# The product of values and attention weights moves from VectorE's part loop to GpSimd, one tile between every two gathers

## The reference

```python
k_e = k[src] + e                    # e = edge features @ We
v_e = v[src] + e
alpha = einsum('ehd,ehd->eh', q[dst], k_e) / sqrt(D)
a = exp(alpha - segment_max(alpha, dst)[dst])
attn = a / segment_sum(a, dst)[dst]
out = segment_sum(attn[:, :, None] * v_e, dst)
```

## Time and profile before

| | |
|---|---|
| median of 3 runs | 5776.57 us |
| profiled execution | 5767.75 us, span 5765.9 us |
| attention gathers begin, end | 1820.4 us, 3115.1 us |
| POOL busy | 3351.3 us (58%) |
| DVE busy | 3076.6 us (53%) |
| PE busy | 3952.0 us (69%), mean granted clock 0.79 |

### The profile page before, as it was taken

One profiled execution on the slowest core, in us unless ns is written; L12 is line 12 of the kernel. 1 busy time (PEld: TensorE's weight loads), 2 busy tenths in 40 slices (PEclk: granted clock), 3 DMA queues, 4 the chain that ended last, 5 costly groups with the idle time before them and its releaser, 6 DMA issues. The chain is left out here.

```text
span 5765.9 us, 96432 instructions
## 1 busy us (share of the span) xinstructions
PE 3952.0 (69%) x24005; PEld 3074.7 (53%) x24006; DVE 3076.6 (53%) x9411; ACT 1420.4 (25%) x3648; POOL 3351.3 (58%) x4762
## 2 busy tenths in 40 slices
PE   1000586779996666677666539998998777777774
PEld 0000353446666566666665526665666666666664
DVE  7887510121115578888887641123114566666667
ACT  0002100010003144454444340002002233333333
POOL 7778988840003888888886220000000688888887
PEclk6555798889998888998997669999999655555555
DMA  9961342346554676676776115544552333333332
GB/s 373 368 227 51 104 156 101 123 129 195 189 167 132 182 210 203 204 233 201 212 221 176 40 59 192 190 139 143 191 189 75 97 92 92 92 92 92 92 92 76
DMA packets 537349, 892.82 MB, mean 155 GB/s; under 512 B 92522, under 2 KB 392140, under 8 KB 530910
## 3 DMA queue, kind: packets, MB, share of 16 engines
q1 hardware_dynamic: 420894, 611.37, 33.0%
q0 software_dynamic: 106912, 224.30, 14.6%
q10 hardware_dynamic: 9376, 55.32, 2.6%
HBM read 732.14 MB, written 158.57 MB: 154 GB/s over the span
## 5 line engine op out<-in xcount | busy, mean ns | idle before, releaser
L381 POOL DMA_INDIRECT work<-tab_gate,src_col x832 | 798.1, 959 | 1272.4 <-DMA tab_gate<-logits 1138.0
L1222 POOL DMA_INDIRECT work<-tab_kv,src_col x832 | 848.5, 1020 | 758.4 <-DMA tab_kv<-hw 589.2
L829 PE MATMUL ps<-hw 128*128 128x384 bf16 x5096 | 873.6, 332 | 108.5 <-DMA hw<-d_adj 62.5
L829 PE MATMUL ps<-hw,work 128*128 128x384 bf16 x5096 | 865.7, 331 | 81.4 <-DMA work<-d_adj 81.4
L501 POOL DMA_INDIRECT d_adj<-logits,address x782 | 800.6, 1024 | 172.3 <-issue 163.7
L869 DVE TENSOR_TENSOR work<-work,ps 128x128 f32 (+1 forms) x208 | 59.8, 288 | 1486.1 <-ACT work L861 1466.0
L829 PEld LDWEIGHTS ps<-hw 128*128 128x128 bf16 x5096 | 504.0, 99 | 451.1 <-issue 62.6
L829 PEld LDWEIGHTS ps<-hw,work 128*128 128x128 bf16 x5096 | 504.5, 99 | 415.7 <-issue 95.8
L861 ACT ACTIVATE work<-ps 128x128 f32 x208 | 57.7, 278 | 1845.6 <-PE ps L829 1845.6
L1737 PE MATMUL ps<-logits,work 128*128 x1664 | 342.9, 329 | 212.5 <-ACT work L1705 210.5
L1737 PEld LDWEIGHTS ps<-logits,work 128*128 128x128 f32 x1664 | 325.7, 291 | 294.7 <-issue 294.7
(11 more groups left out here) (404 smaller groups left out, 7298.7 us busy)
## 6 DMA issues: line engine op xcount, KB each, us to landing
hw<-d_adj SPq DMA_DIRECT2D x104, 800.0 KB
work<-d_adj SPq DMA_DIRECT2D x104, 800.0 KB
d_adj<-acc SPq DMA_DIRECT2D x52, 1568.0 KB, 21.5
hw<-d_adj SPq DMA_DIRECT2D x104, 768.0 KB
work<-d_adj SPq DMA_DIRECT2D x104, 768.0 KB
work<-attr_dram SPq DMA_DIRECT2D x832, 64.0 KB
d_value<-work SPq DMA_DIRECT2D x208, 256.0 KB
hw<-d_value SPq DMA_DIRECT2D x208, 256.0 KB
```

Source lines behind the costliest of these rows:

```text
L381: pool.indirect_dma_start(rows[:, r * U + u, 0:width], None, table, bass.IndirectOffsetOnAxis(sources[:, at:at + 1], 0)).then_inc(rows_in[ ...
L829: last = nc.tensor.matmul(at, adj_half[2 * s + hf][:, k, :], xs[:, b, :], start=b == 0, stop=b == BLOCKS - 1)
L1222: pool.indirect_dma_start(rows[:, r * U + at % U, 0:KV], None, tab_kv, bass.IndirectOffsetOnAxis(src_col[:, at:at + 1], 0)).then_inc(rows_ ...
```

## The change

`weigh_dve` is gone. The product is made by `weigh_part` on POOL, in two forms: in the tail on a whole part as before, and inside `att_pool` on one tile (128x128) behind every gather. While part n is gathered, part n-39 is weighed: its first tile waits for `exp_ready` and `value_in`, the last one signals `msg_ready`. From part 39 on the product stands where the pause stood; parts 0 to 38 and part 207 have no part to weigh, and only the first 39 keep their pauses. PE waits for `msg_ready` in both places.

```diff
-        def weigh_dve(dve, of, turn, r):
-            at, wide = weighed(dve, of, turn, r)
-            nc.vector.tensor_tensor(at, at, wide, ALU.mult).then_inc(sem("msg_weighed"), 1)
-
-        ATT_FILLS = STEPS
+        def weigh_part(pool, m, tiles):
+
+            first, last = tiles
+            r = m % PARTS
+            k = stretch_of(m)
+            p = m - FIRST_PART[k]
+            if first == 0:
+                pool.wait_ge(sem("exp_ready"), FIRST_PIECE[k + 1])
+                pool.wait_ge(value_in[r], 16 * (m // PARTS + 1))
+            n = last - first
+            at = msg_att[:, r * U + first:r * U + last, 0:D].rearrange("p u (h d) -> p u h d", h=HEADS)
+            wide = part_weights(k, p // PARTS, p % PARTS)[:, first:last, :]
+            ins = pool.tensor_tensor(at, at, wide.unsqueeze(3).broadcast_to((P, n, HEADS, HEAD_DIM)), ALU.mult)
+            if last == U:
+                ins.then_inc(sem("msg_ready"), 1)
+
+        ATT_FILLS = WEIGH_BACK * U
 ...
-                    pool.wait_ge(sem("paced"), SPREAD + at)
-                    pool.memset(pause, 0).then_inc(sem("paced"), 1)
+                    if 0 <= m < TAIL_PART:
+                        weigh_part(pool, m, (u, u + 1))
+                    elif m < 0:
+                        pool.wait_ge(sem("paced"), SPREAD + paced)
+                        paced += 1
+                        pool.memset(pause, 0).then_inc(sem("paced"), 1)
 ...
-                pe.wait_ge(sem("msg_weighed"), m + 1)
+                pe.wait_ge(sem("msg_ready"), m + 1)
 ...
-                m, of, turn, rm = part_of(k, i, r, WEIGH_BACK)
-                if summed_in_loop(k, m):
-                    weigh_dve(dve, of, turn, rm)
```

More of the change, by code:

```diff
@@ L1215, in att_pool @@
+        ATT_FILLS = WEIGH_BACK * U
         def att_pool(pool):
+            paced = 0
             pool.wait_ge(sem("table_out"), KV_TABLE)
             for n in range(ALL_PARTS):
-                r = n % PARTS
+                r, m = n % PARTS, n - WEIGH_BACK
                 if n >= PARTS:
                     pool.wait_ge(sem("kv_done"), n - PARTS + 1)
-                for at in range(n * U, (n + 1) * U):
-                    pool.indirect_dma_start(rows[:, r * U + at % U, 0:KV], None, tab_kv,
+                for u in range(U):
+                    at = n * U + u
+                    pool.indirect_dma_start(rows[:, r * U + u, 0:KV], None, tab_kv,
@@ L1226, in att_pool @@
                 if n == PARTS - 1:
                     pool.memset(acc_flat[:], 0.0).then_inc(sem("sums_zeroed"), 1)
+            assert paced == ATT_FILLS
         def tail_pool(pool):
             for m in range(TAIL_PART, ALL_PARTS):
-                k = stretch_of(m)
-                at, wide = weighed(pool, k, (m - FIRST_PART[k]) // PARTS, m % PARTS)
-                pool.tensor_tensor(at, at, wide, ALU.mult).then_inc(sem("msg_ready"), 1)
+                weigh_part(pool, m, (0, U))
         def weights_act(act, m, of, turn, r):
@@ L1380, in sums @@
                 pe.wait_ge(sem("win_added"), (m - PARTS + 1) * U + TURN)
-                pe.wait_ge(sem("msg_ready"), i * PARTS + r + 1)
+                pe.wait_ge(sem("msg_ready"), m + 1)
                 pe.wait_ge(sem("msg_weights"), m + 1)
```

## The result

The changed kernel took 5862.07 us (median of four runs, 5858.7 to 5866.01), the kernel before 5778.57 us beside it (5767.75 to 5786.07). The ratio is 1.0146, 95% interval 1.0129 to 1.0164: slower, by 84 us where 25 were forecast, and 4 us above the range. The profiled execution's span is 5855.7 us, 89.8 longer than before. The gathers of the attention pass begin at 1821.0 and end at 3201.1 us, so the pass lasts 1380.0 us against 1294.7: 85 of the 90 us are in it.

A forecast was written before the change was run, and what follows sets the result against it. The prediction took POOL's own work to be the attention pass's length, with DVE waiting. Its terms, 24 - 20 + 25 - 4 = +25 us on a median of 5776.57, gave 5802 us; the range was 5735 to 5858 us.

The forecast's parts named there:

- rival 4: Attention pass: DVE was the bound, so its relief of 115 us would count; at most 38.5 us back, 5738 us; chance 0.03.
- POOL's pauses become products: POOL in the attention pass: 672 memsets of 0.329 us become products of 0.365 us, +24 us (bounds -43 and +68).
- Relief of the gathers: POOL's gathers: fewer are lengthened once DVE loses line 1211, -20 us (bounds -42 and 0).
- New collisions: POOL's products meeting DVE's two-input line 1408 wait 0.34 us on average, +25 us (bounds 0 and +92).
- Boundaries: Between stretches: a slower POOL loses its extra time out of its wait for DVE's scores, -4 us (-10 to 0).
- New waits: The product's two waits, ahead of the part's other gathers, cost nothing; +10 us if the cover is gone.
- Rival 3: Locked phases: line 1408 keeps falling on a product in each part, +92 in place of +25, 5869 us; chance 0.12.
- Rival 1: The small POOL product is cheap, 0.265 us with next to no fixed part: sum -42, 5735 us; chance 0.20.
- Rival 2: Even exchange: product 0.34 us, line 1211 to blame for most long gathers (-30): sum -2, 5775 us; chance 0.24.

The follow-up runs named there:

- x1: Kernel before, with 672 of its POOL pauses replaced by a 128x128 product on a spare buffer, DVE keeping its own product: 5885.56 us, ratio 1.0189.
- x2: Kernel before, with the same 672 pauses made longer memsets (128x364), about as long as the product: 5822.01 us, ratio 1.0079.
- x3: Changed kernel, with POOL's product in the pass on 64 of the 128 columns of a tile: 5803.18 us, ratio 1.0045.
- w2: Changed kernel, with one 128x512 product behind a part's last gather in place of four small ones: 5813.12 us, ratio 1.0063.
- y4: Kernel before, with 672 pauses replaced by copies of 128x128, on a slower chip: 6366.62 us, ratio 0.9861 to the kernel before there.
- x4: Changed kernel, with DVE's one-hot matrix (line 1417) made by four one-input instructions instead of one with two SBUF inputs: 5833.28 us, ratio 1.0098.

## Why the prediction was wrong in size

- **What bounds the kernel: right.** POOL's account is the pass, before and after; DVE's 115 us were worth nothing as work, and rival 4 is out. x1, x2, x3 and w2 show the pass following POOL's account.
- **"POOL's pauses become products": this term failed.** Forecast +24 us, measured 93. Two parts: the product is 0.413 us instead of 0.365, so 672 x (0.413 - 0.329) = 56 and not 24. The length was inside its bounds (0.265 to 0.43), but I took the middle of two guesses for the fixed part, 0.10 from the memset and 0.186 from the select, where x3 measured 0.195. The fixed part of the instruction with an input was the nearer row. The term as a whole is above its top bound of +68, because the other 37 us were in no term. An exchange was costed as the difference of two durations, but the gather behind a product takes 0.989 instead of 0.952 us (25 us), and the product starts 0.018 us behind its gather, the memset at once (12 us). x1 shows both with nothing else changed, x2 that length does not cause the first, and y4 that a copy, with one input, brings 0.025 of the 0.037 us. That it is the reading, and not another property of these instructions, is not shown.
- **"Relief of the gathers": right in kind, larger than forecast.** Forecast -20 with bounds -42 and 0, measured -35. Time over the undisturbed gather fell from 848.5 - 832 x 0.952 = 56 to 838.4 - 156 x 0.952 - 676 x 0.989 = 21 us; between x1 and the changed kernel the gathers' sum falls by 30. The Trainium skill (SBUF — State Buffer, Who interferes with whom) infers that descriptor generation is spared by such instructions. The relief, and the 9.9 us that gathers lose in x4 with line 1417 on one input, show that a gather is held up, so the prediction was right to keep the term; its sentence that the 1.42 us decides against the page goes too far. In the kernel before, 158 gathers take over 0.03 us more than the usual time, and 157 of them begin while such an instruction or a scan of DVE runs (41 of 42 in the changed kernel; the one left is the first gather of the pass in both). 121 gathers saw one begin only later than 0.15 us behind their own start, and none of these took 0.02 us more. So a gather is held near its start, and the rest of it runs beside such instructions undisturbed. A gather also reads its row numbers from SBUF (`src_col`), and no run separates that reading from the descriptors.
- **"New collisions": right mechanism, other parts.** Forecast +25; the products take 313.5 - 672 x 0.413 = 36 us over their undisturbed time, nearly all in 117 that last over 0.5 us. Of these 107 stand beside line 1417 and have 21.5 us of it, 0.20 each where 74 of 0.34 were forecast, and x4 takes 21 us away by changing line 1417 alone. The other ten stand beside scans and have 14 us, which the prediction had put into its next term. So the nearness of 36 to 25 is in part luck.
- **"Boundaries" and "New waits":** the wait for scores fell by 11.7 us (forecast 4, at most 10), and the products did not wait for their values at all, as costed.
- Sum: 93 - 35 + 36 - 12 = +82 for the pass, measured +85. The failed term alone is 69 us off; the larger relief and the waits took 23 of that back, and the collisions added 11.
- **The rivals.** Rival 3 names 5869 us, close to the result, which is luck: its 92 us for the collisions are 36. Half of its cause is there, though. The 117 long products lie in 113 of the 168 parts, 78 of them on the part's fourth tile, so the phases are locked in part; but each costs 0.20 us beside line 1417 and not 0.55. Rival 1 needed a product below 0.328 us, and x3 shows that even 0.304 would not have been enough. Rival 2's 0.34 us was further off than the forecast's 0.365; the estimate by the Trainium skill (GPSIMD Engine Reference, 3.1 Elementwise) gives the same 0.34 against 0.413 measured.
- **The sign holds for the kind of chip it was timed on.** On the two slower chips the change is 2.6 to 2.9% faster. The prediction rests on the profile of a chip where POOL bounds the pass, and could not speak of the other kind.

## What to carry to other kernels

Where one engine's instructions make up the pass, write its account by rows (busy, idle ahead, issue, waits) and cost an exchange with its neighbours: here the instruction behind and the gap ahead made 37 of 93 us. Take the fixed part of a small instruction from a row with the same kind of inputs, since a memset's is too low for a product. And a filler on the engine that sets the time may cost less than its length: the pause of 0.33 us cost 0.19, because the gap ahead of the next gather is 0.30 us without it and 0.16 with it.

## What the runs showed of the hardware

- A gather's time depends on what POOL ran just ahead of it: 0.946 us behind another gather, 0.952 behind a memset, 0.977 behind a copy, 0.989 behind a product (medians). In x2 a longer memset leaves it at 0.952, and in w2 the undisturbed gathers behind the 128x512 product take 0.99 as well, so the length ahead does not matter. The cause is not known.
- Two gathers in a row have 0.30 us between them, a gather behind a memset or product 0.16.
- This product on POOL, on 128 partitions, costs about 0.195 us and 1.69 ns a column (64, 128 and 512 columns), a memset 0.10 to 0.11 us and 0.83 ns a column (128 to 512 columns).
- In the kernel before and the changed one, a gather was held up only where a scan or an instruction with two SBUF inputs was already running on DVE at its start (157 and 41 gathers), not by one that began later than 0.15 us behind it.
- The hold is mutual. In w2 the one-hot line of DVE has a mean of 1.09 us where it takes 0.69 undisturbed. 88 of its 208 last over 0.8 us (median 1.73); each of them overlaps a 128x512 product of POOL and ends 0.56 us behind that product's end, and the gather that follows is held up in turn. The last three lines show one case:

```profile
L1419 DVE TENSOR_TENSOR work<-iota,rels 128x512 f32<-128x512 f32 x208 | 226.8, 1091 | 0.5
```

```profile
2331.79 1.08 POOL L1215 TENSOR_TENSOR hw<-hw 128x512 f32<-128x512 f32 x1
2332.33 1.09 DVE L1419 TENSOR_TENSOR work<-iota,rels 128x512 f32<-128x512 f32 x1
2333.02 1.26 POOL L1230 DMA_INDIRECT work<-tab_kv,src_col  x1 [0.16 <-issue]
```

- Between two kinds of chip the kernel before differs by 11 to 12% and the changed one by 7%, and a change can have either sign.
